# A decoder layer on one core: the hand-written orders of its first part are rearranged and its first load is split

## The reference

```
x = x + linear_attention(LN(x))        # 16 heads of 16; elu(q)+1, elu(k)+1; biases on q, k, v and out
x = x + softmax(where(mask, -inf, scores * LN(x))) # (ctx Wq + bq)(ctx Wk + bk)^T / 8, with ctx of 256 x 64 per batch
x = x + ffn(LN(x))                     # Hadamard transform, up and gate (1024), silu, Hadamard, down
```

## Time and profile before

| | us |
|---|---|
| median of 3 runs | 133.11 (133.09 to 133.22) |
| profiled execution, own time | 133.7 |
| its span | 131.9 |
| TensorE busy | 125.2 (95%) |
| VectorE busy | 79.7 (60%) |
| ScalarE busy | 75.5 (57%) |
| GpSimd busy | 69.2 (52%) |

### The profile page before, as it was taken

One profiled execution on the slowest core, in us unless ns is written; L12 is line 12 of the kernel. 1 busy time (PEld: TensorE's weight loads), 2 busy tenths in 40 slices (PEclk: granted clock), 3 DMA queues, 4 the chain that ended last, 5 costly groups with the idle time before them and its releaser, 6 DMA issues.

```text
span 131.9 us, 2612 instructions
## 1 busy us (share of the span) xinstructions
PE 125.2 (95%) x974; PEld 116.4 (88%) x974; DVE 79.7 (60%) x202; ACT 75.5 (57%) x162; POOL 69.2 (52%) x89
## 2 busy tenths in 40 slices
PE   6999999997899999999999999999999999999991
PEld 2249799887779999899999999999999999999990
DVE  1279967695995886899796576861626411232211
ACT  1487639965566489866563784458396630354500
POOL 2200999599999999655370344362225360055510
PEclk9999999999999999999999999999999999999999
DMA  4999975000000000000000200000200000200011
GB/s 123 309 327 377 399 247 181 0 0 2 5 2 0 0 0 7 0 0 0 5 0 0 80 0 5 2 0 0 85 0 0 2 0 5 80 0 0 0 35 50
DMA packets 4353, 7.68 MB, mean 58 GB/s; under 512 B 560, under 2 KB 2096, under 8 KB 4212
## 3 DMA queue, kind: packets, MB, share of 16 engines
q1 hardware_dynamic: 4334, 7.50, 16.6%
q10 hardware_dynamic: 6, 0.01, 0.0%
HBM read 6.46 MB, written 1.05 MB: 57 GB/s over the span
## 4 chain that ended last, share of the span: by engine, by line
PE 71%; POOL 13%; ACT 5%; DVE 3%; DMA 3%; issue 2%; POOLq 0%; ACTq 0%
PE bank L1123 35%; PE bank L1136 17%; POOL wug L309 4%; PE bank L1025 3%; POOL rstd L263 3%; PE bank L1003 3%; DMA x_res<-in_x 3%; PE bank L1109 3%; PE bank L1087 2%; POOL wd_a L303 2%; POOL hs L275 1%; PE bank L1059 1%; PE bank L1069 1%; PE bank L1095 1%; PE bank L1049 1%
## 5 line engine op out<-in xcount | busy, mean ns | idle before, releaser
L1123 PE MATMUL bank<-xh_home,wug 128*128 128x256 f32 x384 | 49.5, 285 | 0.0
L1123 PEld LDWEIGHTS bank<-xh_home,wug 128*128 128x128 f32 x384 | 47.1, 191 | 0.7 <-issue 0.4
L314 POOL TENSOR_TENSOR hs<-front,hs 128x256 fp32r<-128x256 f32 x32 | 24.2, 761 | 33.0 <-ACT hs L527 33.0
L518 ACT ACTIVATE front<-bank,vecs 128x256 f32<-128x256 f32 x32 | 15.1, 474 | 20.2 <-PE bank L1123 20.1
L825 DVE SCALAR_TENSOR_TENSOR front<-bank,sc_up,front 128x256 f32<-128x256 f32 x32 | 15.2, 481 | 18.2 <-ACT front L518 18.2
L1136 PE MATMUL bank<-wdh,hs 128*128 128x256 f32 x192 | 23.7, 283 | 0.0
L1136 PEld LDWEIGHTS bank<-wdh,hs 128*128 128x128 f32 x192 | 23.3, 191 | 0.0
L527 ACT CAST hs<-front 128x256 fp32r<-128x256 f32 x32 | 12.8, 401 | 4.0 <-DVE front L825 4.0
L1025 PE MATMUL bank<-wqkv,xT 128*128 128x256 f32 x96 | 14.1, 287 | 0.1
L261 POOL TENSOR_SCALAR veps<-mv 128x2 f32<-128x2 f32 x12 | 2.3, 193 | 21.3 <-DVE mv L647 20.7
L1025 PEld LDWEIGHTS bank<-wqkv,xT 128*128 128x128 f32 x96 | 12.3, 188 | 1.2 <-ACT xT L436 0.7
(11 more groups left out here) (105 smaller groups left out, 194.4 us busy)
## 6 DMA issues: line engine op xcount, KB each, us to landing
wd_a<-in_w_d SPq DMA_DIRECT2D x1, 1024.0 KB, 8.7
front<-in_w_ug SPq DMA_DIRECT2D x2, 512.0 KB, 9.9
back<-in_w_ug SPq DMA_DIRECT2D x2, 512.0 KB, 4.6
out<-x_res SPq DMA_DIRECT2D x8, 128.0 KB, 1.9
wd_b<-in_w_qkv SPq DMA_DIRECT2D x3, 256.0 KB, 5.0
x_res<-in_x SPq DMA_DIRECT2D x1, 512.0 KB, 6.6
x_res<-in_x SPq DMA_DIRECT2D x1, 385.0 KB, 3.9
back<-in_ctx_t SPq DMA_DIRECT2D x1, 260.0 KB
```

Source lines behind the costliest of these rows:

```text
L314: g.tensor_tensor(hs[:, 1, n % JB, :], sg[:, n % RING, :], hs[:, 0, n % JB, :].bitcast(F32), ALU.subtract)\
L518: a.activation(sg[:, n % RING, :], B("GU", n)[:, 0:SEQ], ACT.Silu, scale=vecs[:, V_WSUG + JB + j:V_WSUG + JB + j + 1]).then_inc(s["sg"], 1)
L1123: ins = mm(dst[:, n * SEQ:(n + 1) * SEQ], wug[:, wa, k, at_col + j * P:at_col + (j + 1) * P], xh[b][:, xb, k, :], start=(i == 0), stop=(i ...
```

## The change

Seven edits, all ahead of the first FFN product:

- A new first load c_0 of 65 rows (65 x 386 floats) holds the two projection matrices and the context of batch 0. It lands in a part of the tile kvs that is free at that time. The x load has only the identity and x, and is issued second. The context load has the other three batches.
- u is projected in three pieces, of 256, 256 and 512 columns. On TensorE u(0), u(1) and the scores of batch 0 come ahead of T1(0), and u(2) behind it. The scores of batch 0 leave their place between Q(0) and T1(1). mx, SC(0) and SC(1) use the eighth bank.
- Warm-up: five products ahead of mx, two behind it, two more behind SC(0). The operand of zeros is filled behind two tiny fills.
- The bias load is issued by SyncE, behind the K weights.
- ScalarE: one_rows behind u_copy; u_hi(1) and ctx_hi(1) ahead of the K weights' high part; ctx_hi(2) ahead of exp_k(0); mask_bias behind xT_hi(2) and no longer ahead of ug_hi(0).
- VectorE: ln_stats(1, 1) behind w_lo(1); u_lo(1) behind bias_lo(1); ln_stats(1, 3) ahead of at_lo(0).
- GpSimd: add_ob(1) behind shift_of(3, 0).

```diff
-HEAD = (("mx", 0), ("u", 0), ("T1", 0), ("u", 1), ("K", 0), ("V", 0), ("Q", 0), ("SC", 0), ("T1", 1), ("ST", 0),
+HEAD = (("mx", 0), ("u", 0), ("u", 1), ("SC", 0), ("warm", 0), ("T1", 0), ("u", 2), ("K", 0), ("V", 0), ("Q", 0), ("T1", 1), ("ST", 0),
...
+            sp.dma_start(c_first, c_0).then_inc(ld["c0"], 16)
             sp.dma_start(first[:, 0:X_AT + ST * HID], x[:, 0:X_AT + ST * HID]).then_inc(ld["x0"], 16)
-            sp.dma_start(ctxT, ctx_t).then_inc(ld["ctx"], 16)
+            sp.dma_start(ctxT[:, SEQ:], ctx_t).then_inc(ld["ctx"], 16)
             sp.dma_start(qkv_raw[:, 0], w_qkv[:, 0]).then_inc(ld["wk"], 16)
+            sp.wait_ge(s["bias_zero"], 1)
+            sp.dma_start(bias_raw[ROW_HI:BIAS_ROWS:ROW_LO, :], bias).then_inc(ld["bias"], 16)
...
@@ GpSimd
-            g.memset(junk, 0.0).then_inc(s["junk"], 1)
             g.memset(mhalf[:, :], -0.5)
             g.memset(neg1[:, :], -1.0).then_inc(s["fills"], 1)
+            g.memset(junk, 0.0).then_inc(s["junk"], 1)
...
-            ctx_lo(0)
             ctx_lo(1)
+            ctx_lo(2)
...
-            add_ob(1)
             butterfly(1, 0)
             rstd_of(3, 0)
             shift_of(3, 0)
+            add_ob(1)
             butterfly(1, 1)
@@ ScalarE
-            act.wait_ge(s["bias_zero"], 1)
-            act.dma_start(bias_raw[ROW_HI:BIAS_ROWS:ROW_LO, :], bias).then_inc(ld["bias"], 16)
...
+            mx_copy()
+            u_copy()
             one_rows()
-            mx_copy()
+            u_hi(1)
             bias_hi(K_COLS)
+            ctx_hi(1)
             w_hi("wk", 0)
-            u_copy()
             xT_hi(0)
-            u_hi(0)
             w_hi("wv", 1)
             w_hi("wq", 2)
             bias_hi(Q_COLS)
+            ctx_hi(2)
             exp_k(0)
-            u_hi(1)
-            ctx_hi(0)
-            ctx_hi(1)
+            u_hi(2)
...
             exp_k(1)
-            mask_bias()
             ug_hi(0)
             at_hi(0)
             xT_hi(2)
+            mask_bias()
             exp_q(1)
@@ VectorE
             bias_lo(0, K_COLS)
-            u_lo(0)
             w_lo(1)
+            ln_stats(1, 1)
             w_lo(2)
             bias_lo(1, Q_COLS)
-            ln_stats(1, 1)
+            u_lo(1)
             elu_k(0)
             v_add(0)
-            u_lo(1)
+            u_lo(2)
             ln_stats(1, 2)
...
             v_add(1)
+            ln_stats(1, 3)
             at_lo(0)
             xT_lo(2)
-            ln_stats(1, 3)
```

More of the change, by code:

```diff
@@ L32 @@
 BANKS = 8
-WARM, WARM_MORE = 8, 2
+WARM, WARM_MORE, WARM_LAST = 5, 2, 2
 MASKED = 3.0e35
@@ L36 @@
 SW = P + HPB
-X_AT = P + 2 * CTX1
+X_AT = P
 RING = 4
@@ L44 @@
 K_COLS, Q_COLS = slice(0, HID), slice(HID, 2 * HID)
-U_COLS = (slice(SEQ, 2 * SEQ), slice(2 * SEQ, 4 * SEQ))
+U_COLS = (slice(0, SEQ), slice(SEQ, 2 * SEQ), slice(2 * SEQ, 4 * SEQ))
 UG_ORDER = (0, 2, 1, 3)
@@ L75, in banks_of @@
     return [(group, i, t) for t in range(2)] if group in ("NUM", "Y") else [(group, i, 0)]
+IN_SCORES = (("mx", 0, 0), ("SC", 0, 0), ("SC", 1, 0))
 def schedule():
@@ L86, in schedule, with decoder_kernel @@
         order += [g for j in (JB, JB + 1) for name, i in SIDE.get((b, j), ()) for g in banks_of(name, i)]
-    return [g for g in order if g not in (("SC", 0, 0), ("SC", 1, 0))]
-def decoder_kernel(nc, x, ctx_t, w_qkv, bias, w_o, w_ug, w_d, vec, row, mask_ss, mask_key, const, out):
+    return [g for g in order if g[0] != "warm" and g not in IN_SCORES]
+def decoder_kernel(nc, c_0, x, ctx_t, w_qkv, bias, w_o, w_ug, w_d, vec, row, mask_ss, mask_key, const, out):
     bank_of, turn_of = {}, {}
@@ L93, in decoder_kernel @@
         bank_of[group], turn_of[group] = n % (BANKS - 1), n // (BANKS - 1)
-    for b in range(ST):
-        bank_of["SC", b, 0], turn_of["SC", b, 0] = BANKS - 1, b
+    for n, group in enumerate(IN_SCORES):
+        bank_of[group], turn_of[group] = BANKS - 1, n
     stack = ExitStack()
@@ L108, in decoder_kernel @@
         first = sb("x_res", [P, X_AT + TILES * HID])
-        ident, wx = first[:, 0:P], first[0:CTX, P:X_AT]
+        ident = first[:, 0:P]
         xs = first[:, X_AT:].rearrange("p (t d) -> p t d", d=HID)
@@ L182, in decoder_kernel @@
         qkv_raw = wd_b[:, 0:FB * 3, :].rearrange("p (c f) o -> p c f o", c=3)
-        bias_raw = kvs[0:BIAS_ROWS, :, :].rearrange("p b e -> p (b e)")[:, 0:2 * HID]
+        kvs_flat = kvs[:, :, :].rearrange("p b e -> p (b e)")
+        bias_raw = kvs_flat[0:BIAS_ROWS, 0:2 * HID]
+        c_first = kvs_flat[0:CTX1, 2 * HID:2 * HID + 2 * CTX1 + SEQ]
+        wx, ctx0 = c_first[0:CTX, 0:2 * CTX1], c_first[:, 2 * CTX1:]
         bytes_of = score[:, :, :].rearrange("p b s -> p (b s)").bitcast(U8)
@@ L205, in wait_read @@
             eng.wait_ge(read[bank_of[name, i, t]], turn_of[name, i, t] + 1)
-        loads = "x0 x1 x2 cst wk wv wq ctx bias vec row wsd mss mkey wo wd ug0 ug1 ug2 ug3".split()
+        loads = "c0 x0 x1 x2 cst wk wv wq ctx bias vec row wsd mss mkey wo wd ug0 ug1 ug2 ug3".split()
         ld = {n: sem("ld_" + n) for n in loads}
@@ L212, in decoder_kernel @@
                  "stats1 aggr1 nmean1 eps1 rstd1 xn1 nmr1 stats2 aggr2 eps2 rstd2 stats3 aggr3 nmean3 eps3 rstd3 nmr3 xn3 "
-                 "w_hi w_lo bias_hi bias ctx_hi ctx_lo u_first u_hi wo_hi wo_lo msum mbias xb had_ready sc_up "
+                 "w_hi w_lo bias_hi bias ctx_hi ctx_lo u_hi wo_hi wo_lo msum mbias xb had_ready sc_up "
                  "ug_hi ug_lo fly pre_hi pre_lo wd wd_hi "
@@ L273, in ctx_lo @@
                 cols = U_COLS[c]
-                pool.wait_ge(s["ctx_hi"], c + 1)
+                pool.wait_ge(s["ctx_hi"], c)
                 g.tensor_tensor(ctxr[:, 1, cols], ctxT[:, cols], ctxr[:, 0, cols].bitcast(F32), ALU.subtract)\
@@ L401, in u_copy @@
                 wait_full(act, "u", 0)
-                a.copy(u_first, B("u", 0)[0:CTX1, 0:SEQ]).then_inc(s["u_first"], 1)
+                a.copy(u_first, B("u", 0)[0:CTX1, 0:SEQ]).then_inc(read_of("u", 0), 1)
             def u_hi(c):
@@ L406, in u_hi @@
                 cols = U_COLS[c]
-                a.copy(ux[:, 0, cols], B("u", c)[0:CTX1, cols.start - c * 512:cols.stop - c * 512]).then_inc(s["u_hi"], 1)
+                a.copy(ux[:, 0, cols], B("u", c)[0:CTX1, 0:cols.stop - cols.start]).then_inc(s["u_hi"], 1)
             def wo_hi():
@@ L661, in u_lo @@
             def u_lo(c):
-                dve.wait_ge(s["u_hi"], c + 1)
+                dve.wait_ge(s["u_hi"], c)
                 cols = U_COLS[c]
-                if c == 0:
-                    dve.wait_ge(s["u_first"], 1)
-                v.tensor_tensor(ux[:, 1, cols], B("u", c)[0:CTX1, cols.start - c * 512:cols.stop - c * 512],
+                v.tensor_tensor(ux[:, 1, cols], B("u", c)[0:CTX1, 0:cols.stop - cols.start],
                                 ux[:, 0, cols].bitcast(F32), ALU.subtract).then_inc(read_of("u", c), 1)
@@ L959, in done, with warm, warm_last @@
                 ins.then_inc(full[bank_of[name, i, t]], 1)
-            def warm(n):
+            def warm(n, into):
                 for _ in range(n):
-                    mm(bank[BANKS - 1][:, :], junk[:, 0:P], junk, start=True, stop=True)
+                    mm(into[:, :], junk[:, 0:P], junk, start=True, stop=True)
             def weights_product(_):
                 dst = take("mx", 0)
-                pe.wait_ge(ld["x0"], 16)
+                pe.wait_ge(ld["c0"], 16)
                 done(mm(dst[0:CTX1, 0:CTX1], wx[:, CTX1:2 * CTX1], wx[:, 0:CTX1], start=True, stop=True), "mx", 0)
-                warm(WARM_MORE)
+                warm(WARM_MORE, B("T1", 0))
+            def warm_last(_):
+                warm(WARM_LAST, B("T1", 0))
             def project(c):
@@ L973, in project @@
                     wait_read(pe, "mx", 0)
+                if c == 1:
                     pe.wait_ge(ld["ctx"], 16)
-                dst = take("u", c)
-                done(mm(dst[0:CTX1, :], mx[:, :], ctxT[:, c * 512:(c + 1) * 512], start=True, stop=True), "u", c)
+                dst, cols = take("u", c), U_COLS[c]
+                done(mm(dst[0:CTX1, 0:cols.stop - cols.start], mx[:, :], ctxT[:, cols] if c else ctx0, start=True, stop=True), "u", c)
             def scores(b):
                 if b == 0:
-                    pe.wait_ge(s["u_first"], 1)
+                    wait_read(pe, "u", 0)
                 else:
-                    wait_read(pe, "u", b // 2)
+                    wait_read(pe, "u", b // 2 + 1)
                     pe.wait_ge(s["ctx_lo"], b // 2 + 1)
@@ L990, in scores @@
                     if b == 0:
-                        ins = mm(into, ctxT[:, rows_of], u_first, start=True, stop=True)
+                        ins = mm(into, ctx0[:, rows_of], u_first, start=True, stop=True)
                         continue
@@ L1162, in down @@
                     done(block_products(i, JB - 1), "Y", b, i)
-            steps = {"mx": weights_product, "u": project, "T1": turn1, "SC": scores, "K": k_proj, "V": v_proj, "Q": q_proj,
```

(11 more changed lines are left out.)

## The result

| | us |
|---|---|
| before, median of 4 runs | 133.17 (133.09 to 133.48) |
| changed, median of 4 runs | 135.11 (134.59 to 136.37) |
| ratio | 1.0126, 95% interval 1.0072 to 1.018 |
| changed, profiled execution | 134.85, span 133.1 |
| changed once more (e10), 6 runs | 134.97 (134.36 to 136.1), ratio 1.0109 (1.0056 to 1.0162) |

The forecast was 132.4 with a range up to 133.5. Medians are of all runs, and ratios leave out the runs that are over 1.5% above the fastest of their kernel, so where a kernel's runs fall into two groups the ratio is mostly of the lower one.

What follows compares the result with a forecast made beforehand. It took VectorE's list to set K(1), GpSimd's never-dry queue to hold TensorE from 20 to 38.9 us, and TensorE to be full afterwards. +0.20 - 0.92 = -0.72 from median 133.11 gave 132.4; range 131.6 to 133.5.

Steps and rivals of the forecast that it cites:

- New work of TensorE ahead of T1(0): Head of TensorE's queue: fewer warm-ups plus the new products end T1(0) at 8.3 to 8.5; cost 0, bounds 0 to 0.3.
- The array's clock: Rival, head: rate rises only behind SC(0), T1(0) ends at some 10.5, +1.5, so 134.6 us; chance 0.04.
- Batch 0's scores at zero: Between Q(0) and T1(1): the 1.03 removed becomes TensorE idle time ahead of K(1), since VectorE's list is only permuted; zero.
- The split load, +0.2: First loads: x0 issued second, behind c0, delays batch 0's statistics, T1(0) and K(1) by 0.2; bounds 0 and 0.44.
- mask_bias, -0.92: ScalarE, mask_bias behind xT_hi(2), with ln_stats(1, 3) earlier on VectorE: GpSimd's shift for batch 3 at 26.57, not 27.49.
- add_ob(1) at zero: GpSimd, add behind T3(0)'s shift: up to 0.49 won at 39 us, given back by 59; zero, bounds 0 and 0.49.
- Collisions: Rival: VectorE and GpSimd instructions exclude each other, as batch 1's root beside w_lo(2) and bias_lo; costs 0.5, 132.9 us; chance 0.20.

Runs made afterwards that it cites:

- e10: The changed kernel itself run again with no edit, beside its variants on one chip: 134.97 us, ratio 1.0109 to the kernel before.
- e1: The changed kernel with eight warm-up products ahead of mx instead of five: 133.44 us, ratio 0.9988 to the kernel before.
- e2: The changed kernel with its nine warm-ups moved: five ahead of mx, four behind it, none behind SC(0): 133.35 us, ratio 0.9967 to before.
- e3: The kernel before with five warm-up products ahead of mx instead of eight, nothing else: 135.18 us, ratio 1.0154.
- e6: The kernel before with nearly all of batch 0's score products left out at their old place: 133.53 us, ratio 1.0001.
- e4: The kernel before with only three order edits (mask_bias, ln_stats(1, 3) and add_ob(1) moved), old head kept: 132.24 us, ratio 0.9905.
- e7: The changed kernel with the mask_bias, ln_stats(1, 3) and add_ob(1) order edits undone, new head kept: 135.02 us, ratio 1.0027 to before.
- e9: The changed kernel with its last two warm-ups between u(0) and u(1) instead of behind SC(0): 133.41 us, ratio 0.996 to before.

## Why the prediction was wrong

The step that failed is *New work of TensorE ahead of T1(0)*, put at 0 with 0.3 for the range. Measured, T1(0) ends at 10.18 and not at 8.3 to 8.5, 2.1 after the kernel before, because the array stayed at its lower level until 12.9. The sum costed "five warm-up products instead of eight" for its time alone (2.25), as a filler of a wait, and took the rates behind it from a trace in which the level had risen.

The mechanism stood among the rivals, as *The array's clock*: T1(0) at 10.5 and the time at 134.6; measured 10.2 and 135.11. It got a chance of 0.04, and the range ended at 133.5 without it. What it named as the danger was TensorE standing between the five warm-ups and c0; that break was only some 0.1 (five products of 0.43 each from 1.37 on, mx at 3.62), and the level stayed low all the same. What was done until 6 differs in another way: ten full products before, now seven, and 65-row products in the place of the others. e1 to e3 show that the three products matter: taken from the old kernel they cost 1.5%, given back to the new one they win 1.2 to 1.4% (ratios 1.0109 and 1.0126 against 0.9988). They don't decide alone: in e10 the level rose at 5.1 with only five ahead of mx.

The Trainium skill ("TensorE: Matmul & The Clock Gate", Part 1) says that the slow level is the default and that the point of the rise varies from run to run, by about half a us. That it varies agrees: one program, once up at 5.1, once at 12.9. Every trace here starts at the lower level, too. The size of the variation doesn't agree, and the measurement decides.

*Batch 0's scores at zero*: right (e6, 1.0001 with 0.4 us either way, where 1.03 was the other bound). VectorE's list from xT_lo(0) to xT_lo(1) took 7.99 (10.84 to 18.83), before 8.03 (8.72 to 16.75): a permutation.

*The split load, +0.2*: not settled. The statistics start at 4.40, before at 4.68, which is the other sign. Over all traces they start at 4.05 to 4.69 with the old loads (six, median 4.37) and at 4.26 to 5.08 with the split ones (seven, median 4.53): 0.16 later, but executions of like heads differ by more. c0 had landed by 3.62, the 3.6 taken.

*mask_bias, -0.92*: right on a head in time: 26.66 in e4 and 26.83 in e10 for 26.57 and 26.77. Under the late head the three edits are worth between 0.15 and 0.7 (e7). The prediction took 0.92 off each rival as if the terms added. For the clock rival the number came out near (2.1 lost and 0.9 back in the trace), but the reason is doubtful: e7's trace has 1.8 lost at xT(1) (18.51 against 16.75) and 1.3 at the end (130.45 against 129.16) with the old orders, so some comes back without the edits. By its time e3, late with the old orders and the old head, loses 2.1 (1.0154).

*add_ob(1) at zero*: somewhat too low. T3(0) doesn't wait, and GU(4) waits 0.30 on VectorE as foreseen, but 0.2 to 0.3 are left at the end, inside the bounds of 0 and 0.49.

*Collisions*: they are there, but GpSimd pays. Timeline of the changed kernel:

```profile
13.49 0.66 DVE L687 TENSOR_TENSOR wqkv<-wd_b,wqkv 128x512 fp32r<-128x512 f32 x1
...
13.66 0.54 POOL L271 TENSOR_SCALAR veps<-mv 128x2 f32<-128x2 f32 x1 [7.14 <-DVE mv L655]
...
14.19 0.41 DVE L666 TENSOR_TENSOR bias_r<-kvs,bias_r 1x256 fp32r<-1x256 f32 x1
14.29 0.87 POOL L273 TENSOR_TENSOR rstd<-veps,mhalf 128x2 f32<-128x2 f32 x1
```

w_lo(2) and bias_lo keep their lengths; GpSimd's two take 0.54 and 0.87 instead of 0.19 and 0.70. It had slack there: its shift for batch 1, at 15.47, waits 0.31 for ScalarE's nmean.

What stays open: why the level rises so much later in some executions than in others of the same program; how often it rises in time in the changed kernel (one execution of two seen in a profile); what share of the spread in the other kernels' runs is this, the kernel before among them (10 of its 75 runs beside the variants have a span of 133.2 or more, where e3's profiled one lies, and 60 one of 131.2 to 132.1); and whether e9's two products helped.

## What to carry to other kernels

Dummy products at the start are not filler for a wait: whoever shortens them, or puts small products in their place, must ask when the array's rate rises, by the length of like products in the timeline and not by a busy share. A saving on one engine's queue is worth what the next wait leaves of it; find the list whose sum doesn't change. And terms found on a head that is in time may not hold on a late one: measure the parts of a change apart and together.

## What was not expected of the hardware

The granted clock column shows 1.00 while 512-column bf16 products start 0.43 apart, the rate of the lower level, and f32 products of 256 columns 0.43 apart, where they are 0.22 apart later. The rise fell at 5.1 to 6.7 in ten of the profiled executions and at 12.9 to 14.9 in three, and at 5.1 and 12.9 in one and the same program. The last store of 128 KB was waited for 1.3 in twelve profiled executions and 2.7 in one.
